# Residual state without its row mean, the mean as an extra product column, and a new order in the source passes

## The reference

```
h = relu(layernorm(x));  x = x + spmm(h), twice hopped        # each message times edge_weight
h = relu(layernorm(x));  x = x + D^-1/2 (A + I) D^-1/2 (h @ W) + b
h = relu(layernorm(x));  x = x + relu((h + A h) @ W1.T + b1) @ W2.T + b2
h = relu(layernorm(x));  m = relu([h[src], h[dst], edge_attr] @ mW1 + mb1) @ mW2 + mb2
                         x = x + relu([h, segment_sum(m, dst)] @ uW1 + ub1) @ uW2 + ub2
layernorm(x) = (x - mean(x)) / sqrt(var(x) + 1e-5)            # over the 64 features, no scale, no shift
```

## Time and profile before

| | us |
|---|---|
| median of 3 runs (lowest, highest) | 5288.51 (5279.80, 5291.18) |
| the profiled execution's own time | 5290.87 |
| its span, first to last instruction | 5289.1 |
| granted TensorE clock over the span | 0.752 of full |
| busy in the span: PE, DVE, POOL, ACT | 3658.4, 3415.4, 3419.2, 1775.4 |

### The profile page before, as it was taken

How to read it: one execution, slowest core, us unless ns; L and a number is a source line. 1 busy time by engine, 2 the same in 40 slices (tenths; PEclk the granted TensorE clock), 3 DMA queues, 4 the chain that set the end, 5 groups by cost and what they waited for, 6 DMA issues and landing times. The chain is left out here.

```text
span 5289.1 us, 68034 instructions
## 1 busy us (share of the span) xinstructions
PE 3658.4 (69%) x18258; PEld 2927.2 (55%) x18258; DVE 3415.4 (65%) x7361; ACT 1775.4 (34%) x3984; POOL 3419.2 (65%) x2949
## 2 busy tenths in 40 slices
PE   3766666666289999766666667777537777787874
PEld 2444344444189999644444455555426666666763
DVE  5444344444155555488888869999857777777772
ACT  1533444334111111133333333343314433343441
POOL 2777777777578888755545345665654667676654
PEclk9766666666555555588888888898868888888886
DMA  4233323332344444323323223333332322223220
GB/s 142 42 53 53 53 42 53 53 53 38 78 74 69 69 69 69 40 90 102 106 95 110 81 89 127 128 126 134 129 116 63 103 69 79 93 71 102 63 66 19
DMA packets 323086, 424.92 MB, mean 80 GB/s; under 512 B 206679, under 2 KB 224573, under 8 KB 322428
## 3 DMA queue, kind: packets, MB, share of 16 engines
q1 hardware_dynamic: 146956, 335.86, 18.0%
q0 software_dynamic: 176000, 87.72, 13.5%
HBM read 245.54 MB, written 212.59 MB: 87 GB/s over the span
## 5 line engine op out<-in xcount | busy, mean ns | idle before, releaser
L852 POOL DMA_INDIRECT ga<-table,isl x784 | 841.2, 1073 | 271.8 <-issue 231.4
L889 POOL DMA_INDIRECT hop<-acc,osl x392 | 635.7, 1622 | 194.6 <-issue 130.1
L925 POOL DMA_INDIRECT xu<-acc,osl x392 | 620.3, 1582 | 141.6 <-issue 100.5
L1105 PE MATMUL tp<-us,wide 128*128 128x64 f32 x1568 | 341.1, 421 | 348.4 <-DVE us L1754 348.4
L1105 PEld LDWEIGHTS tp<-us,wide 128*128 128x128 f32 x1568 | 336.6, 332 | 354.9 <-issue 354.9
L988 POOL DMA_INDIRECT out_x<-acc,osl x392 | 427.9, 1091 | 133.8 <-issue 114.7
L852 POOL DMA_INDIRECT ga<-xu,isl x392 | 413.3, 1054 | 139.0 <-issue 116.8
L1157 PE MATMUL tp<-us,wide 128*128 128x64 f32 x1568 | 416.8, 422 | 120.0 <-DVE wide L1913 120.0
L1045 PE MATMUL mm<-bias,rows 128*128 128x512 bf16 (+1 forms) x616 | 246.1, 399 | 323.2 <-ACT zx L1379 195.0
L852 POOL DMA_INDIRECT ga<-in_x,isl x392 | 392.0, 1000 | 119.7 <-issue 93.5
L1120 PE MATMUL tp<-xw,cc 128*128 128x394 f32 x784 | 398.1, 602 | 96.0 <-ACT found L1402 95.7
(11 more groups left out here) (320 smaller groups left out, 8951.2 us busy)
## 6 DMA issues: line engine op xcount, KB each, us to landing
wide<-xu SPq DMA_DIRECT2D x84, 448.0 KB, 3.8
zx<-key_rows SPq DMA_DIRECT2D x28, 896.0 KB, 4.6
out_x<-wide SPq DMA_DIRECT2D x56, 448.0 KB, 2.7
table<-acc SPq DMA_DIRECT2D x56, 448.0 KB, 2.4
xin<-xs SPq DMA_DIRECT2D x56, 448.0 KB, 3.7
wide<-table SPq DMA_DIRECT2D x56, 448.0 KB
xu<-in_x SPq DMA_DIRECT2D x25, 1000.0 KB, 5.5
hop<-zeros SPq DMA_DIRECT2D x1, 12544.0 KB, 35.6
```

Of the source, the lines that this page charges most:

```text
L852: nc.gpsimd.indirect_dma_start(o[:, g, :], None, table, bass.IndirectOffsetOnAxis(idx[:, g:g + 1], 0)).then_inc(s, 16)
L889: nc.gpsimd.indirect_dma_start(hop, bass.IndirectOffsetOnAxis(osl[b][:, g:g + 1], 0), acc[b][:, g, :], None, bounds_check=hop_max, oob_is_ ...
L925: nc.gpsimd.indirect_dma_start(xu, bass.IndirectOffsetOnAxis(osl[b][:, g:g + 1], 0), acc[b][:, g, :], None, bounds_check=all_max, oob_is_e ...
L1105: t = nc.tensor.matmul(o[:, g * D:g * D + D], equal[b][:, c, (g % 2) * P:(g % 2) * P + P], us[b][:, c, :], start=n == 0, stop=n == 1)
```

## The change

**What it computes otherwise.** The state that goes from layer to layer is kept centred. The weights and biases of the products that end in the residual (`wg`, `w2b`, `b1g`, `b2b`) are centred over their 64 outputs in the preparation, and their mean becomes a 65th column (`C = D + 1`). A product then gives the centred part, which DVE adds to the centred state, and one number per row, which DVE adds to `mean_row` (128 x 14). Layer norms 2 and 3 lose their sum and their subtraction; layer norm 1 keeps both, now in place (`lane_x`, `ga`, `gx`). The output needs the mean again: ACT puts it back with one `ACTIVATE` a row, `Identity` with the mean as bias, 14 a unit (`dense_mean_back`, and in the last stage in place of the copy at L1555). In the last stage the mean is also masked and summed along the running rows (`tensor_tensor_scan`).

```diff
+            for t, n in ((wg[:, :], 2), (w2b[:, :], 2), (bias_f[:, BG, 0:HB * C], HB), (bias_f[:, B2, 0:HB * C], HB)):
+                by_node = t.rearrange("p (r c) -> p r c", c=C)
+                mean, own_part = by_node[:, :, D:C], by_node[:, :, 0:D]
+                link(V.tensor_reduce(by_node[:, :, D], own_part, X, ALU.add))
+                link(V.tensor_scalar(by_node[:, :, D], by_node[:, :, D], 1.0 / D, None, ALU.mult))
+                link(V.scalar_tensor_tensor(own_part, mean.broadcast_to([P, n, D]), -1.0, own_part, ALU.mult, ALU.add))
...
+            def by_pair(o, src_, weights, k, signal, key):
+                for s in range(2):
+                    at = 512 * s
+                    nc.tensor.matmul(o[:, at:at + HB * C], rows3[:, :], bias[:, k, 0:HB * C], start=True, stop=False)
+                    for j in range(4 * s, 4 * s + 3):
+                        c = at + (2 * j - s * HB) * C
+                        nc.tensor.matmul(o[:, c:c + 2 * C], src_[:, j * P:j * P + P], weights, start=False, stop=False)
+                    c = at + (1 - s) * 6 * C
+                    t = nc.tensor.matmul(o[:, c:c + C], src_[:, 3 * P:4 * P], weights[:, s * C:s * C + C],
+                                         start=False, stop=True)
+                signal.raise_by(t, key)
...
+            def dense_mean_back(j, q):
...
+                act.wait_ge(*dn.taken.at(j, ("x3", q)))
...
+                for g in range(G):
+                    t = nc.scalar.activation(lane_o[q][:, g, :], lane_y[q][:, g, :], ACT.Identity,
+                                             bias=mean_row[q][:, g:g + 1])
+                dn.copied.raise_by(t, ("y3", q))
...
                 elif n == "x3":
                     dve.wait_ge(*dn.second.at(j, ("h2", q)))
-                    ins = V.tensor_tensor(flat(lane_y[q]), flat(lane_y[q]), mm[q][:, 0:W], ALU.add)
+                    V.tensor_tensor(by_half(mean_row[q][:, :]), by_half(mean_row[q][:, :]), mean_part(mm[q]), ALU.add)
+                    ins = V.tensor_tensor(halves(lane_y[q]), halves(lane_y[q]), centred_part(mm[q]), ALU.add)
```

In the last stage:

```diff
-                        tt.acc_ready.raise_by(nc.scalar.copy(flat(acc[b]), flat(x3[b])), ("a", b))
+                        for g in range(G):
+                            t = nc.scalar.activation(acc[b][:, g, :], x3[b][:, g, :], ACT.Identity,
+                                                     bias=mean_run[b][:, g:g + 1])
+                        tt.acc_ready.raise_by(t, ("a", b))
...
-                    hd = layer_norm(own, tt, j, "d2", B2K, [full(xd[b]) for b in B2K], [full(h[b]) for b in B2K],
-                                    [[xm[b]] for b in B2K])
+                    hd = layer_norm(own, tt, j, "d2", B2K, [full(xd[b]) for b in B2K], [full(h[b]) for b in B2K])
...
+                        own.wait(ms[b], fs[b], ends[b], *([runs[0]] if b else []))
+                        before = 0.0 if i is None and b == 0 else mean_run[1 - b][:, 0:1]
+                        runs[b] = raised(tt.centred, j, ("d3", b),
+                                         V.tensor_tensor_scan(mean_run[b][:, ::-1], st[b][:, 0, ::-1],
+                                                              mean_row[b][:, ::-1], before, ALU.mult, ALU.add))
```

**The order of the source passes** is new on PE, ACT and DVE; SP's and POOL's is as it was. On PE and ACT the products of `h2`, lane 1, move from the end of a pass to the start of the next. On DVE the beginning of a pass now reads:

```diff
+                if k == 0:
+                    source_mean(own, i, 1)
                 if k == 1:
                     source_sum(own, i, 1)
-                dense_mean(own, l, "l2", 0)
-                dense_mean(own, j, "l1", 1)
+                dense_spread(l, "l2", 0)
+                dense_inverse(own, l, "l2", 0)
+                dense_normal(own, l, "l2", 0)
                 if k == 1:
                     source_scale(own, i, 1)
+                dense_add(l, "x3", 1)
+                if k == 1:
                     source_sum(own, i, 0)
-                dense_centre(own, l, "l2", 0)
-                if k == 1:
                     source_scale(own, i, 0)
+                if k == 0:
+                    source_mean(own, i, 0)
```

More of the change, by code:

```diff
@@ L22 @@
 HB = G // 2
+C = D + 1
 ROWS = P * T
@@ L453, in gnn @@
+            hidden = Ticks(sem("dense_hidden"), [("h2", 1), ("h2", 0), ("even", 1), ("odd", 1), ("even", 0), ("odd", 0)],
+                            [("h2", 1), ("h2", 0), ("even", 1), ("odd", 1), ("even", 0), ("odd", 0)])
+            second = Ticks(sem("dense_second"), [("h2", 1), ("h2", 0), ("h3", 1), ("h3", 0)],
+                            [("h2", 1), ("h2", 0), ("h3", 1), ("h3", 0)])
         dn = Dense
@@ L1224, in source_product @@
                 pe.wait_ge(*f.copied.at(i, ("v", b)))
-                by_row(tp[b], [flat(vt[b])], wg[:, :], BG, f.product, ("v", b))
+                by_pair(tp[b], flat(vt[b]), wg[:, :], BG, f.product, ("v", b))
             def sums_span(k):
@@ L1724, in _, with layer_norm @@
             dve.sem_inc(s_prep, 1)
-            def layer_norm(own, f, i, n, lanes, xs, hs, ready, scale=None, free=None, final=None, before=None):
+            def layer_norm(own, f, i, n, lanes, xs, hs, ready=None, scale=None, final=None, before=None, centre=None):
                 marks = {}
-                for q in lanes:
-                    own.wait(*ready[q])
-                    marks[q] = own.did(V.tensor_reduce(st[q][:, 0, :], xs[q], X, ALU.add))
-                for q in lanes:
-                    own.wait(marks[q])
-                    f.centred.raise_by(V.scalar_tensor_tensor(full(lane_c[q]), stat(q, 0), -1.0 / D, xs[q],
-                                                              ALU.mult, ALU.add), (n, q))
-                    if free is not None:
-                        free(q)
+                centre = centre or xs
+                if ready is not None:
+                    for q in lanes:
+                        own.wait(*ready[q])
+                        marks[q] = own.did(V.tensor_reduce(st[q][:, 0, :], xs[q], X, ALU.add))
+                    for q in lanes:
+                        own.wait(marks[q])
+                        f.centred.raise_by(V.scalar_tensor_tensor(centre[q], stat(q, 0), -1.0 / D, xs[q],
+                                                                  ALU.mult, ALU.add), (n, q))
                 for q in lanes:
@@ L2100, in one_pass @@
+                dense_centre(own, j, 0)
+                dense_spread(l, "l3", 0)
+                if between is not None:
+                    sums_span(between)
+                dense_spread(j, "l1", 1)
                 if k == 1:
                     source_add(i, 0, first)
-                dense_spread(j, "l1", 1)
-                dense_inverse(own, l, "l3", 1)
+                dense_spread(j, "l1", 0)
+                dense_inverse(own, l, "l3", 0)
+                dense_normal(own, l, "l3", 0)
@@ L2117, in one_pass @@
                 dense_inverse(own, j, "l1", 1)
-                if k is not None:
-                    source_mean(own, k, i, 1)
-                dense_centre(own, l, "l3", 0)
+                dense_inverse(own, j, "l1", 0)
                 if k is not None:
                     source_spread(k, i, 0)
-                    source_centre(own, k, i, 1)
-                    source_inverse(own, k, i, 0)
-                dense_spread(l, "l3", 0)
-                if k is not None:
-                    source_normal(own, k, i, 0, first)
@@ L2128, in one_pass @@
-                dense_inverse(own, l, "l3", 0)
-                dense_inverse(own, j, "l1", 0)
-                dense_normal(own, l, "l3", 0)
                 dense_normal(own, j, "l1", 1)
-                dense_add(l, "out", 1)
                 if k is not None:
                     source_spread(k, i, 1)
+                    source_inverse(own, k, i, 0)
+                    source_normal(own, k, i, 0, first)
+                dense_add(l, "out", 1)
+                dense_normal(own, j, "l1", 0)
@@ L2135, in one_pass @@
+                if k is not None:
                     source_run(own, k, i, 0, first)
@@ L2240, in last_pass @@
                         xm[b] = own.did(V.tensor_tensor(full(xd[b]), full(xd[b]), cols(last, tcol(j, b)), ALU.mult))
-                    ends = {}
+                        own.wait(ms[b])
+                        dve.sem_inc(s_passed, 1)
+                        ms[b] = own.did(V.tensor_tensor(mean_row[b][:, :], mean_row[b][:, :],
+                                                        last[:, bass.ds(tcol(j, b), G)], ALU.mult))
+                        fs[b] = own.did(V.tensor_copy(st[b][:, 0, :], more[:, bass.ds(tcol(j, b), G)]))
+                    ends, runs = {}, {}
                     for b in B2K:
```

280 lines of the change are left out of this document (144 added, 136 removed).

## The result

| | median us (lowest, highest) |
|---|---|
| before, 4 runs | 5286.82 (5279.80, 5291.18) |
| after, 4 runs | 5348.72 (5347.05, 5353.81) |
| after / before | 1.012, 95% interval 1.010 to 1.014 |

The change makes the kernel 62 us slower. The profiled execution of the changed kernel has a span of 5352.0 us (before: 5289.1) and a granted clock of 0.742. Each is one line of the program: its count, duration min/median/max in ns, first and last start. The first two are the row sum of `ga` and `source_sum` in the changed kernel, then the running sum of the last stage, after and before, then `source_sum` before; the row sum before is the earlier trace rows.

What follows compares the result with a forecast made beforehand. DVE bounds both source loops, no engine the last stage. Span 5289.1 + 5 (preparation) + 238 (first loop) + 5 (edges) - 15 (passes between) - 66 (second loop) - 71 (last stage) = 5385; total 5387 us, range 5310 to 5450.

Steps and rivals of the forecast that it cites:

- Chain and head: First source loop: lane 1's row sum at the head waits for gathers; pass 73.0 us for 54.7, +238 in all.
- the ring through `ga`: First source loop: `source_normal` of lane 0 over stores and gathers to the head, 46.0 us, plus 27.0 back to `source_normal`.
- PE's clock at the head: First source loop: PE's first products run slow after idling, so head to `source_normal` takes 27.0 us, not 23.6.
- Edges and passes between: Edges of the first source loop: +16 and -11, together +5 us; two passes between the source loops: -15 us.
- Second loop: Second source loop: gathers bind, not DVE; 51.5 us a pass for 57.5, -66 us over eleven passes.
- the six units between the two sums: Second source loop: six DVE operations between the two `source_sum`s put 6.0 us on top of 45.5 us for the gathers.
- Last stage: Last stage: 5.1 us less a period, -71 us over 14 periods, bounds -20 and -130.
- ACT's 28 instructions: Last stage: two ACT copies become 28 instructions of 0.21 us each, 6.0 us, +4.2, delaying the update's copies.
- A: First source loop: the pass's head does not wait; -99 us in place of +238, total 5045 us; chance 0.06.
- B: First loop: shortest wait, 69 us a pass; last stage: all 12 us a period gained; total 5238 us; chance 0.06.
- C: Last stage: ACT's instructions and cooled PE eat the gain; gather pairs stay long; total 5470 us; chance 0.08.

Runs made afterwards that it cites:

- s3: Kernel before, loops written out, with lane 1's row sum moved to the head of the first source loop's passes; 6315 us, ratio 0.996 to the kernel before.
- s5: Changed kernel, loops written out; `source_normal` of lane 0 later in the first source loop, mean not put back in the last stage; 6224 us, ratio 0.984.
- s4: Changed kernel, loops written out; lane 1's row sum late, the two `source_sum`s together, ACT's update copy between the lanes' mean instructions; 5933 us, ratio 0.937.
- s2: Changed kernel with the loops of both source stages and the last stage written out; 6115 us, ratio 0.970 to the kernel before.

## Why the prediction was right, point by point

The forecast was 5387 us, 96 us more of span; measured were 5349 and 62.9. The mechanism is the one forecast. Of the 33 us between the two, 18 are in the last stage, where the gain was put too small, and 12 in the first loop. In the stages around the second loop, 10 us more than forecast in one and 7 us less in another nearly cancel, which is luck.

- **Chain and head.** Right: the term that decides is the ring through `ga`, 46.0 + 27.0 forecast, 44.3 + 27.7 measured in the pass shown, 44.8 + 27.2 in the mean. The 1.7 us came from gathers that take 35.6 us in place of 37.4; that DVE, standing still, disturbs them less is a guess that no run tested. Shown by s3 (added to the old kernel), s5 (longer way, longer pass) and s4 (moved away, wait gone), all three with the loops written out and beside late issue. I bounded this at 69 to 75.5; 71.9 lies inside. From head to head the 13 passes added 225.6 us, not 238 (2273.5 to 2983.1 before, 2266.7 to 3201.9 after).
- **PE's clock at the head.** The 3.35 us product and the waits of 1.7 us twice (expected 2.6 and 1.0) are there. By the Trainium skill, "TensorE: Matmul & The Clock Gate", Part 1, an idle array is clocked down; the trace agrees, with 3.35 us after 22 us of idle time and 1.77 us later (the prediction calls the two "the same product"; they are two products of one size). These waits lie on the way from the head to `source_normal`, so they are part of the ring, some 3 of its 72 us. They do not make the other 44 us: s5 lengthened the way and these stayed.
- **Edges and passes between.** The sums of the first three stretches are +229 against +233, but two errors cancel: 12 us less in the first loop, 10 us more here. The addition at the borders of the two passes between, in the earlier trace rows for the kernel before, separates edge and passes; in the changed kernel it is:

```profile
3250.16 1.08 DVE L2039 TENSOR_TENSOR wide<-wide,mm 128x896 f32<-128x896 f32 x1
3344.12 1.08 DVE L2039 TENSOR_TENSOR wide<-wide,mm 128x896 f32<-128x896 f32 x1
```

  The edges are as forecast: from the last head to the first of these 48.3 us, where it was 31.4 (+17, forecast +16), and the first head 6.8 us earlier, of which the preparation took 3.8 back (DVE's first row sum of the first layer starts at 112.3 in place of 108.5 us; forecast +5), so -10.6 for -11. The two passes between are what I had wrong: 94.0 us in place of 100.2, -6 where I had -15.
- **Second loop.** 51.1 us a pass against 51.5, bound by gathers as said. That the six units between the two sums cost anything could not be tested: in s4 issue bound that loop. Open.
- **Last stage.** The size that was off most. I said "5.1 a period"; it was 6.8. `d2` and `s3` gave 6.3 (the additions ahead of them start at 4844.71 and 5017.31, 61.5 and 61.0 us into the period, so -0.5 there and -6.8 at its end), where I had 4.3. Up to the reciprocal of `d3` nothing is gained: its 3.6 us were eaten by the update's delay, 3.8, which I had put at 2.5. The stretch from there to the additions ahead of `d2` gave 0.7 more. PE's idle time ahead of the relu fell from 9.37 to 5.66 us as forecast, but for another reason: the work before it ended later, the relu came no sooner.
- **ACT's 28 instructions.** 6.79 us, or 0.2425 each; I took 0.21. Here the Trainium skill, "VectorE: DVE Perf Modes", section "The TRN2 errata", was nearer: 224 + 64 cycles, an estimate of 240 ns, by that page. The measurement settles it.
- **Rivals.** A (no wait at the head) is excluded. B and C each named one end: the last stage gave more than I took, 6.8 us, but not the 12 us of B, and C's loss of that gain and its long gathers did not come. Between the second loop and the first running sum, where I had 0, another 7 us went; no run looks into that.

What stays open: why PE, ACT and DVE stand idle at the loops' ends in all the later runs and not in the first, and why PE's clock stays up over the same idle time in some periods and falls in others. That s4's moves beat the kernel before where issue is prompt was not measured either; my estimate from the chain (44.3 + 7.1 us) is passes of 51 us for 71.9.

## What to carry to other kernels

Before moving an instruction that reads gathered or loaded data, find what last used its buffer, and add up the ring from there over the transfers to the instruction; whatever stands between the two on the in-order engine is part of the round. An instruction at the head of a queue makes all behind it wait, so a reader of late data belongs as near as possible ahead of the work that frees its buffer. Where an engine that is not the bound gets many small instructions, look at what its queue holds next: copies that started 2.2 us late cost PE its higher clock too, in most periods.

## What the runs showed of the hardware that was not expected

- The same kernel took 5287 us in one measurement and 6308 to 6477 in others, 19 to 23% more. In the traces of the slower ones PE, ACT and DVE stand idle with nothing to wait for, such as 2.43 us between single transposes on PE and 1.7 us between two instructions of DVE's running sum, while POOL's gathers keep their pace (35.4 us a pair of lanes). A change judged under one condition (1.012) comes out the other way under the other (0.985).
- The 14 instructions of a running sum take 5.75 us inside an engine's loop and 4.45 us written out, the same operations on the same tiles. Late issue has no part in it: in the first trace of the kernel before, too, the pass written out ahead of the loop has 4.45 us and the loop 5.84.
- A product of eight 512-column matmuls took 3.27 us after PE had idled 0.23 us. After 2.92 us of idle time it took 4.97 us in every period of the changed kernel's first trace, but 3.27 us in the first four of 13 periods of s2, where the granted clock stayed at 1.0.
